# Upper norm at the front of a step, and the last block's dense part of MLP layer 1 computed in step 7, in a DLRM tower kernel

## The reference

```
x = layer_norm(dense @ Wd.T)                            # 128 per sample
y = layer_norm(einsum('bnd,ed->bne', e, Ws))            # 26 rows of 128
y = layer_norm(einsum('bne,pn->bep', y, Wsi))           # 32 per e
T = concat([x, y^T])                                    # 33 rows of 128
Z = T @ T^T ; Zflat = lower triangle of Z               # 528
z = layer_norm(Zflat @ Wl.T)[:, :384]                   # "upper" layer
h = relu(concat([z, dense]) @ W_top1 + b_top1)          # 384 + 256 -> 512
h = relu(h @ W_top2 + b_top2)                           # 512 -> 256
out = h @ W_top3                                        # 256 -> 1
```

## Time and profile before

| what | value |
|---|---|
| three executions | 182.54, 183.28, 187.37 us; median 183.28 |
| the profiled execution | 184.72 us; span from the first to the last instruction 182.9 us |
| mean granted TensorE clock in it | 0.944 |
| TensorE busy | 148.9 us (81% of the span), weight loads 105.9 |
| VectorE, ScalarE, GpSimd busy | 117.3, 85.9, 105.0 us |
| chain of work that ended last | GpSimd 36%, TensorE 34%, issue 14%, ScalarE 6%, DMA 5%, VectorE 3% |

### The profile page before, as it was taken

The page is one execution under the profiler, slowest core; times in us unless marked ns, Lnnn a source line. Parts: engine busy times, 40 slices in busy tenths (PEclk is TensorE's granted clock), DMA queues, the critical chain, the costliest instruction groups (busy, mean ns, idle before and its releaser), DMA issues.

```text
span 182.9 us, 4658 instructions
## 1 busy us (share of the span) xinstructions
PE 148.9 (81%) x1865; PEld 105.9 (58%) x1865; DVE 117.3 (64%) x279; ACT 85.9 (47%) x229; POOL 105.0 (57%) x108
## 2 busy tenths in 40 slices
PE   0474584658994979968896999999699999998995
PEld 0363262444452558635566977765398865596674
DVE  3799508794959999992969069968942898600000
ACT  3001324572634776752655256638604764522262
POOL 2778778787878787778777877788774000000000
PEclk9998869995899999999997899999969999999999
DMA  5714241325186633321255313212452102422000
GB/s 128 220 24 110 50 135 35 82 27 195 34 249 127 80 63 44 60 54 27 53 76 71 48 28 56 56 29 57 68 78 41 34 0 48 61 36 34 0 4 0
DMA packets 38520, 12.01 MB, mean 66 GB/s; under 512 B 34113, under 2 KB 35265, under 8 KB 38498
## 3 DMA queue, kind: packets, MB, share of 16 engines
q1 hardware_dynamic: 33586, 8.24, 20.2%
q0 software_dynamic: 3328, 3.41, 10.8%
q10 hardware_dynamic: 1584, 0.05, 0.5%
HBM read 9.46 MB, written 2.23 MB: 64 GB/s over the span
## 4 chain that ended last, share of the span: by engine, by line
POOL 36%; PE 34%; issue 14%; ACT 6%; DMA 5%; DVE 3%; SPq 1%; ACTq 0%
POOL rows L302 36%; PE pV L341 4%; PE pU L381 4%; PE pU L408 4%; PE pU L422 3%; PE pT L351 3%; PE pA L325 2%; PE pU L434 2%; PE pA L381 2%; PE pZ L364 2%; DMA zr<-zscr 1%; DMA rows<-in_tables,idx 1%; PE pA L318 1%; DMA idx_in<-in_index 1%; ACT ujunk L615 1%
## 5 line engine op out<-in xcount | busy, mean ns | idle before, releaser
L302 POOL DMA_INDIRECT rows<-in_tables,idx x104 | 104.7, 1007 | 34.3 <-issue 31.4
L756 DVE TENSOR_TENSOR prod<-pA,rows 128x384 f32<-128x384 f32 (+1 forms) x16 | 9.4, 591 | 28.8 <-PE pA L325 28.8
L780 DVE TENSOR_TENSOR t<-pT,bias 128x512 f32<-128x512 f32 x32 | 20.6, 684 | 4.3 <-PE pT L351 4.3
L584 ACT ACTIVATE t<-t 128x512 f32<-128x512 f32 x32 | 19.5, 629 | 7.4 <-DVE t L780 7.1
L795 DVE TENSOR_TENSOR T<-t,trs 128x512 f32<-128x512 f32 x32 | 22.2, 694 | 1.1
L318 PE MATMUL pA<-const,rows 128*128 128x128 f32 x52 | 9.0, 288 | 15.8 <-DMA rows<-in_tables,idx 15.8
L341 PE MATMUL pV<-wexp,srow 128*64 128x192 f32 (+4 forms) x256 | 21.4, 313 | 0.0
L786 DVE TENSOR_REDUCE tss<-t 128x16 f32<-128x512 f32 x32 | 20.4, 677 | 0.1
L325 PE MATMUL pA<-gbd,rowsT 128*128 128x128 f32 x104 | 17.5, 311 | 3.6 <-ACT rowsT L567 3.5
L364 PEld LDWEIGHTS pZ<-T 128*32 128x32 f32 x1024 | 12.2, 112 | 12.3 <-issue 9.8
L341 PEld LDWEIGHTS pV<-wexp,srow 128*64 128x64 f32 x256 | 16.4, 145 | 4.9 <-issue 2.7
(11 more groups left out here) (153 smaller groups left out, 214.0 us busy)
## 6 DMA issues: line engine op xcount, KB each, us to landing
zscr<-zs SPq DMA_DIRECT2D x16, 128.0 KB
rows<-in_tables,idx POOLq DMA_INDIRECT x104, 2.5
wl_sb<-in_wl SPq DMA_DIRECT2D x5, 256.0 KB, 2.9
w_sb<-in_w SPq DMA_DIRECT2D x5, 256.0 KB
dense_sb<-in_dense_t SPq DMA_DIRECT2D x1, 512.0 KB, 4.7
w_sb<-in_w SPq DMA_DIRECT2D x1, 512.0 KB, 4.5
zr<-zscr SPq DMA_DIRECT2D x3, 96.0 KB
const<-in_consts SPq DMA_DIRECT2D x1, 263.0 KB, 3.2
```

The source lines that it names most:

```text
L302: pool.indirect_dma_start(out=rows[:, j, h * D:(h + 1) * D], out_offset=None, in_=tables, in_offset=bass.IndirectOffsetOnAxis(ap=idx[:, 2 ...
L584: a.activation(t2[:, h], t1[:, n % 2, h], ACT.Square).then_inc(t_sq, 1)
L780: v.tensor_tensor(t1[:, n % 2, h], pT[h][:].rearrange("p (a b) -> p a b", b=PJ), bias[:].unsqueeze(1).to_broadcast([P, US, PJ]), ALU.add). ...
```

## The change

Eight edits, which compute the same result:
- In steps 9 and 13 VectorE's `upper_inverse` goes to the front of the step, ScalarE's `upper_scaled` ahead of `mixed`, TensorE's `turn` ahead of `interact`, and ScalarE's `upper_turned` ahead of `interactions`.
- In every step VectorE's `biased` is split: first half, `scaled_rows`, second half.
- In step 7 TensorE computes the dense part of layer 1 for block 3 into pU (`dense_ahead`), behind b1p; VectorE copies it to hd in SBUF; the first upper layer waits for the copy.
- `hidden1_dense(LAST)` goes; the last block's `hidden1` starts its sums itself.
- VectorE adds hd to these sums (`hidden_sum`, into hs), and the last relu1 reads hs in place of PSUM.
- In step 16 TensorE's part 1 of the upper layer of block 2 moves behind the embedding and the interactions of unit 14, with 2 and 3; parts 4 and 5 move behind the interactions of unit 15.
- ScalarE copies the interactions of unit 15 ahead of the norm and the scaling of block 2.

```
@@ PE @@
-                        pe.wait_ge(b1_ready, 1)
+                        pe.wait_ge(hd_sb, 1)
...
+            def dense_ahead():
+                pe.wait_ge(b1_ready, 1)
+                for m in range(H1 // P):
+                    for c in range(USED // P, NK):
+                        got = mm(pU[:, P * m:P * (m + 1)], w1_sb[:, c, P * m:P * (m + 1)],
+                                 dense_sb[:, c - USED // P, P * LAST:P * (LAST + 1)], start=c == USED // P, stop=c == NK - 1)
+                got.then_inc(hd_done, 1)
...
                 if k == LAST:
+                    pe.wait_ge(zs_sb, NU)
+                    pe.wait_ge(t1_sb, 2 * NU)
...
-                                     start=False, stop=c == USED // P - 1, skip_group_check=True)
+                                     start=c == 0, stop=c == USED // P - 1)
...
                 if n < NU:
                     gram(n)
+                if n == 7:
+                    dense_ahead()
...
-                if n == NU:
-                    upper(LAST - 1, [1])
                 if n:
                     embed(n - 1)
...
+                if (k := block_at(n, MLP)) is not None:
+                    turn(k)
...
                 if (k := block_at(n, MLP)) is not None:
-                    turn(k)
                     hidden1_dense(k)
...
                 if n == NU:
-                    upper(LAST - 1, [2, 3, 4, 5])
+                    upper(LAST - 1, [1, 2, 3])
             interact(NU - 1)
+            upper(LAST - 1, [4, 5])
             hidden1_dense(LAST - 1)
             turn(LAST - 1)
-            hidden1_dense(LAST)
             hidden1(LAST - 1)
@@ ACT @@
                 for m in range(H1 // P):
-                    if m == 0 or k == LAST:
-                        act.wait_ge(h1_done, H1 // P * k + (m + 1 if k == LAST else H1 // P))
-                    a.activation(h1[:, m, :], hidden_part(k, m), ACT.Relu, bias=b1p[:, m:m + 1]).then_inc(h1_sb, 1)
+                    got = hidden_part(k, m)
+                    if k == LAST:
+                        act.wait_ge(hs_sb, m + 1)
+                        got = hs[:, P * m:P * (m + 1)]
+                    elif m == 0:
+                        act.wait_ge(h1_done, H1 // P * (k + 1))
+                    a.activation(h1[:, m, :], got, ACT.Relu, bias=b1p[:, m:m + 1]).then_inc(h1_sb, 1)
...
+                if (k := block_at(n, MLP)) is not None:
+                    upper_scaled(k)
                 if n:
                     mixed(n - 1)
-                if (k := block_at(n, MLP)) is not None:
-                    upper_scaled(k)
...
+                if (k := block_at(n, MLP)) is not None:
+                    upper_turned(k)
                 if n >= 2:
                     interactions(n - 2)
-                if (k := block_at(n, MLP)) is not None:
-                    upper_turned(k)
...
+            interactions(NU - 1)
             upper_norm(LAST - 1)
             upper_scaled(LAST - 1)
-            interactions(NU - 1)
             x_row(LAST)
@@ DVE @@
+            def hidden_sum():
+                for m in range(H1 // P):
+                    dve.wait_ge(h1_done, H1 // P * LAST + m + 1)
+                    v.tensor_tensor(hs[:, P * m:P * (m + 1)], hidden_part(LAST, m), hd[:, P * m:P * (m + 1)],
+                                    ALU.add).then_inc(hs_sb, 1)
...
             for n in range(NU + 1):
+                if (k := block_at(n, MLP)) is not None:
+                    upper_inverse(k)
                 if n < NU:
                     row_variance(n)
-                if (k := block_at(n, MLP)) is not None:
-                    upper_inverse(k)
+                if n == 7:
+                    dve.wait_ge(hd_done, 1)
+                    v.tensor_copy(hd[:], pU[:]).then_inc(hd_sb, 1)
                 if n:
-                    biased(n - 1)
+                    biased(n - 1, 0)
                 if n < NU:
                     scaled_rows(n)
                 if n:
+                    biased(n - 1, 1)
                     variances(n - 1)
                     normalised(n - 1)
...
             upper_inverse(LAST)
+            hidden_sum()
```

More of the change, by code:

```diff
@@ L120, in build @@
         b1p = sb("b1p", [P, H1 // P])
+        hd = sb("hd", [P, H1])
+        hs = sb("hs", [P, H1])
         xstat = sb("xstat", [P, NBLK, 6])
@@ L196, in build @@
         w1_ready, b1_done, b1_ready = map(sem, ["w1_ready", "b1_done", "b1_ready"])
+        hd_done, hd_sb, hs_sb = map(sem, ["hd_done", "hd_sb", "hs_sb"])
         gathered = [sem(f"gathered{i}") for i in range(NU)]
@@ L400, in hidden1_dense @@
                     pe.wait_ge(t1_sb, 2 * NU)
-                if k == LAST:
-                    pe.wait_ge(zs_sb, NU)
-                    pe.wait_ge(u_sb, LAST)
                 if k == 0:
@@ L408, in hidden1_dense @@
                         mm(hidden_part(k, m), w1_sb[:, c, P * m:P * (m + 1)], dense_sb[:, c - USED // P, P * k:P * (k + 1)],
-                           start=c == USED // P and (m == 0 or k == LAST), stop=False, skip_group_check=True)
+                           start=c == USED // P and m == 0, stop=False, skip_group_check=True)
             def hidden1(k, part=range(USED // P)):
@@ L773, in scaled_rows, with biased @@
                                 ers[:, 0:2 * count].unsqueeze(2).to_broadcast([P, 2 * count, D]), ALU.mult).then_inc(s_sb, 1)
-            def biased(n):
-                if n >= 2:
+            def biased(n, h):
+                if n >= 2 and h == 0:
                     dve.wait_ge(t_sb, 2 * (n - 1))
-                for h in range(2):
-                    dve.wait_ge(y_done, 2 * n + h + 1)
-                    v.tensor_tensor(t1[:, n % 2, h], pT[h][:].rearrange("p (a b) -> p a b", b=PJ),
-                                    bias[:].unsqueeze(1).to_broadcast([P, US, PJ]), ALU.add).then_inc(t1_sb, 1)
+                dve.wait_ge(y_done, 2 * n + h + 1)
+                v.tensor_tensor(t1[:, n % 2, h], pT[h][:].rearrange("p (a b) -> p a b", b=PJ),
+                                bias[:].unsqueeze(1).to_broadcast([P, US, PJ]), ALU.add).then_inc(t1_sb, 1)
             def variances(n):
```

## The result

The changed kernel takes 189.9 us in the median of four runs (189.23 to 191.59); the kernel before, timed beside it, takes 183.62 us (182.54 to 187.37). The ratio is 1.0385 with a 95% interval of 1.0303 to 1.0468. The forecast was 185.2 us with a range up to 187.8.

The account below looks back on a forecast made before the run. Gathers set the earliest step starts; from about 100 us the chain is TensorE work, with a VectorE and ScalarE detour. Terms 0.75 + 0.4 - 0.1 + 0.6 + 0.3 = +1.95 us gave 185.2 us against 183.28, range 182.0 to 187.8.

Parts of the forecast that it names:

- Cost 0, hidden by that wait: Step 7: the 16 dense matmuls moved there cost nothing, hidden by step 8's wait for its rows.
- the cover: Before step 8: 2.68 us idle waiting for rows, called nearly used up; without it the step-7 work costs about 2.7 us.
- I leave the two clock falls as they are: Steps 9 and 13: the forecast keeps both falls of TensorE's clock; step 13's costs 1.6 us.
- Rival (b): Step 13: the stall closes, znT starts before 131.8, kernel faster at 181.1 us, half form 183.7; together 20%.
- the two terms: Steps 13 and 9: dense matmuls later by +0.75 us and +0.4 us.
- un displaces nothing: Step 9: ScalarE waited for the mixing matmuls before vsb, so only the split counts, +0.4 us.
- The second square in front of znT: Step 13, ScalarE: the second half's square delays znT from 131.81 to 132.55; TensorE idles some 2.2 us.
- Step 16, -0.1 us: Last embedding: srow of unit 15 comes 0.6 us earlier, mix gains 0.3, the embedding 0.1; bounds -0.3 to 0.
- The end, +0.6 us: After the last interactions: znT is later and ScalarE's reads wait for it, +0.6 us; bounds +0.2 (TensorE alone) and +1.0.
- The sum on VectorE, +0.3 us: Last stretch: the last 128x128 sum before relu, 0.27 us plus hand-over, lies in the path; bounds 0.2 and 0.7.
- Rival (c): Behind 150 us: TensorE's clock falls once or twice more, slower at 186.9 or 188.5 us; 13%.
- My list of new gaps: TensorE idle 1.3 us before the last embedding, 1.4 before the last interaction, 0.9 before the L422 matmuls.

Follow-up runs that it names:

- e8: The whole change, split kept, with znT copied between the two squares in steps 9 and 13: 185.46 us, ratio 1.0108.
- e12: The whole change, split kept, with step 7's dense_ahead directly ahead of upper(0) and the hd copy behind the scaled rows: 187.01 us, ratio 1.0264.
- e1: The kernel before with only the last block's dense part moved to step 7, with the copy to hd and sums on VectorE: 186.27 us, ratio 1.0194.
- e4: The changed kernel with both halves of the bias sum ahead of the scaled rows again: 184.18 us, ratio 1.0064.
- e10: The kernel before with only the new end: 183.82 us against 184.51, ratio 1.0119 (0.9983 to 1.0256).
- e9: The kernel before with only the new order of steps 9 and 13 and znT copied ahead of both squares, old end: 181.92 us, ratio 0.9936.
- e7: The change without split or step-7 work, with znT copied ahead of both squares in steps 9 and 13: 182.29 us, ratio 0.9941.
- e5: The change without split or step-7 work, only the new orders of steps 9 and 13 and the end: 183.27 us against 183.22, ratio 1.0022.
- e11: e9 with ScalarE's two copies of the last interaction ahead of the norm's scaling, TensorE's order old: 181.32 us, ratio 0.9934.
- e2: The kernel before with only the bias sum split around the scaled rows, in every step: 188.24 us, ratio 1.0246.
- e6: e4 with dense_ahead directly ahead of upper(0) in step 7 and the hd copy behind the scaled rows: 183.53 us, ratio 1.0006.
- e3: The changed kernel with the last block's dense part back at the end, no sum on VectorE: 186.47 us, ratio 1.001.

## Why the prediction was wrong

**Step 7, "Cost 0, hidden by that wait": wrong.** Its own steps show how. I took b1p from the earlier trace rows at 76.20, and nothing else moved. In the change b1p stands on VectorE behind w1g and the last T, and these behind the roots on ScalarE; it comes at 77.54. (How late it is varies: 5.1 us into the step in the change and 5.2 in e8, 4.0 in e12, all with the split; 4.5 in e1 and e4, without it. So the split is not its only cause.) The copy rowsT on ScalarE was late too, by 1.08 us on TensorE. And dense_ahead put a wait in front of 16 matmuls, so TensorE stood still with all that followed. Waits and work came to 1.08 + 1.67 + 3.62 = 6.4 us, where I had counted some 2 (76.35 to 78.2), and before, the step had 2.68 us to spare: 6.4 - 2.7 = 3.7 us too much, close to the 3.1 us found. I wrote that the cover was "nearly used up, without it ~2.7 us", so the price stood in the text, but nothing was set against the cover: neither the changes that the other edits make to this step, nor a fall of the clock. So the term had three sizes wrong: the arrival of b1p (5.1 us into the step, counted as 3.4), the new matmuls (3.62 us, counted as some 2) and the wait for rowsT (1.08 us, counted as nothing).

And the cover is no fixed number. Five of the kernels below are the kernel before up to step 9, and only its execution differs: their wait for rows ahead of step 8 is 1.77 us (e10), 1.50 (e9), 0.22 (e7) and none (e5, e11), and b1p comes 3.5 to 4.5 us into step 7, where the one trace that I had read has 2.68 and 3.4. Step 8 in e10 and e5:

```profile
82.33 0.63 PE L322 MATMUL pA<-const,rows 128*128 128x128 f32 x4 [1.77 <-DMA rows<-in_tables,idx]
84.56 0.60 PE L322 MATMUL pA<-const,rows 128*128 128x128 f32 x4
```

By these waits 2 us of new matmuls would be hidden in some executions and not in others, even where nothing else changes. e1's cost agrees with this, but no run isolates it.

**"I leave the two clock falls as they are": wrong as a baseline, and this hid the main cost of the split.** The dense matmuls of steps 9 and 13, counted by order over all traces of this case:

| order | idle ahead of them (us) | ran slow | step with full clock | step with a fall |
|---|---|---|---|---|
| as before (before, e1, e10) | 1.41 to 1.42 | 4 of 6 | 9.6 to 9.7 | 11.3 to 11.4 |
| as before, split (e2) | 2.45 | 2 of 2 | | 12.6 to 12.7 |
| new, not split (e4, e5, e6) | 1.30 to 1.44 | 0 of 6 | 9.2 to 9.8 | |
| new, split (the change, e3, e12) | 1.77 to 2.15 | 4 of 6 | 10.4 to 10.7 | 11.4 to 12.3 |
| znT ahead of a square (e7, e8, e9, e11) | at most 0.50 | 0 of 8 | 7.9 to 9.6 | |

The falls are no fixed part of the kernel before: with the same order they were missing in two of six places. And the new order without the split shortens a step only where it spares it a fall: with full clock on both sides it takes 9.2 to 9.8 us against 9.6 to 9.7. The timed runs of e5 show no gain, so what it wins on average is small, and that the order itself keeps the clock up (0 of 6) is suggested and not shown. What the split adds is clearer: at full clock about 0.9 us a step (e12 against e4 and e6), and 1.0 to 1.5 us more with a fall, which is what makes the change so much slower than e4 in these two steps. Rival (b) named the right lever, znT held by the second square, but it expected the change to pull it. Against the kernel before, whose trace had both falls, the two terms came to +0.8 in step 13 (forecast +0.75) and +1.0 in step 9 (forecast +0.4). That the first fits is partly luck, as both traces happen to have the fall. (A slip in the starting point: 136.78 - 133.6 is 3.2 us of lateness, and the idle time and the fall make 3.0 of it, not all of 3.1.) In step 9 "un displaces nothing" failed: un stands ahead of vsb there too, and rowsT is late as well (0.35 us of TensorE's time). The wait for vsb:

```profile
96.73 1.13 PE L355 MATMUL pT<-vsb,wscg 64*128 64x512 f32 x4 [0.39 <-ACT vsb L592]
```

**The second square in front of znT: right, and shown.** un, vsb, the second bias sum and znT came in the order and nearly with the distances given; TensorE idled for 1.79 us where I said 2.2. e2 adds the stall (2.45 us), e8 removes it (0.48 us) with everything else kept. Rival (b) asked for znT ahead of 131.8 and a closed stall; the change did not do this. The stall closes in e9 and shrinks to 0.48 us in e8.

**Step 16, -0.1 us: wrong sign.** The last embedding comes 8.7 us behind step 15's transposes, before 8.1. I counted srow of unit 15 as half a sum earlier. It was not earlier at all: it starts 5.2 us behind step 15's transposes before and after, since the last T of the unit before, and with it the row variance, moved back by as much as srow moved forward. The row before and the row after:

```profile
149.83 0.56 DVE L771 TENSOR_TENSOR srow<-rows,ers 128x384 f32<-128x384 f32 x1
153.57 0.56 DVE L788 TENSOR_TENSOR srow<-rows,ers 128x384 f32<-128x384 f32 x1
```

I also left out what stands in front of vsb on ScalarE. In step 16 that is both squares, the zs copies and the roots of unit 14, and the split makes them all late. The same event in e4 and in e8, which differ in the split here (ScalarE rows of the timeline; step 15's transposes at 144.07 and 144.05):

```profile
151.28 0.57 ACT L592 COPY vsb<-pV 128x512 f32<-128x512 f32 x1
```

```profile
152.10 0.57 ACT L592 COPY vsb<-pV 128x512 f32<-128x512 f32 x1
```

The split costs 0.8 us here. In every trace with the split the last embedding stands 8.66 to 8.67 us behind the transposes, in e4 7.83 us. So the split, whose purpose was an earlier srow, gained nothing in this stretch that could be set against its price.

**The end, +0.6 us: right in mechanism, too large.** The reads on ScalarE's queue left right behind the start of znT (167.97 and 167.91), as I read from the earlier trace rows; SyncE's reads of the same write had left at 166.85. But the path is TensorE's: the block-2 matmuls start 0.57 us behind znT, and the upper ones follow without a wait. From the last interaction this is +0.3 us, my lower bound of +0.2 and not the +0.6 of the reads. The new end as a whole costs about 0.4 us with the step-7 work in (e4: 38.7 us from step 15 to the end, before 38.3) and 0.8 without it (e5 and e10 39.1); these numbers are from traces, and the timed runs of e10 don't settle it.
Of the Trainium skill I had weighed "Advanced Engine Details and Errata", section "Sequencer Loop", by which further engine instructions can be read and queued while the sequencer handles one. Here the reads did not get past a copy that still waited; the row of after agrees with the earlier trace rows.

**The sum on VectorE, +0.3 us: right.** One sum takes 0.29 us (forecast 0.27), the path grew by 0.3.

**Rival (c), more clock falls behind 150 us, did not happen:** the slices of the page show 9 there. This is the line of the page after:

```profile
PEclk9997897999996999889998799999969999999999
```

An additional fall did happen, in step 7, where I had set no gap at all. My list of new gaps came from the end alone. Of these the ones ahead of the last embedding (1.40 us) and the last interaction (0.96 us) are there, and no fall followed.

**What stays open.** e8, with the stalls of steps 9 and 13 mended, is still 1.3 us above e4; 0.8 of it is step 16, the rest may be step 7, and no run separates it. What the step-7 work costs inside the split change is 3.4 us by e3's median and more by its ratio; its place alone (e12) makes up 2.9 us of the medians. Only one trace was taken of each kernel, so the steps of two kernels also differ by what differs from one execution to the next. Nor do the runs tell why the clock falls in one execution and not in another with the same stall (below).

## What to carry to other kernels

Before an operation is split or slid on an in-order engine, list every instruction that stands behind the second half on that engine and on the ones that read it, and look for the one that the bound engine waits for. Here a single copy (znT, 0.46 us) stood behind it, and taking it out from behind was worth 4.4 us. Then ask whether the first half comes earlier at all once the loop has settled: here srow did not.

Work moved into "spare" time needs three looks: whether its input is ready when the spare time begins, how much of the cover the other edits of the same change have already used, and whether the cover is there in more than one execution (here 2.68 us in the trace that was read, and 0 to 1.77 us in five others). And if the kernel before has stalls that cost more than their length, a forecast that holds them fixed misses both what an edit could win and what it throws away.

The parts worth having are the front order with znT ahead of both squares, and the old end or zs first: e9 181.92 and e11 181.32 us, against 184.51 us of the kernel before in that batch. The ratios, 0.9936 and 0.9934, make that a gain of about 1.2 us: clear of 1, but small.

## What the hardware showed that was not expected

The length of a stall does not tell whether TensorE's clock falls. The dense matmuls of steps 9 and 13 ran slow (3.5 to 3.6 us for 16) after 1.42 us of idle time in the kernel before, and at full clock after 1.41 and 1.42 us in step 9 of e1 and e10, which have the same order of work there, and after 1.44 us in e5. Within one execution, e10, step 9 and step 13 differ:

```profile
97.04 2.05 PE L421 MATMUL pU<-dense_sb,w_sb 128*128 128x128 f32 x16 [1.42 <-ACT znT L641]
129.93 3.06 PE L421 MATMUL pU<-dense_sb,w_sb 128*128 128x128 f32 x16 [1.42 <-ACT znT L641]
```

After 1.79 us they ran slow in the change (3.06 us in step 9, part of them at full clock, and 3.58 us in step 13), and at full clock (2.05 us) after 1.77 and 1.79 us in e12. After at most 0.50 us they never ran slow (e7, e8, e9, e11: eight times of eight). In step 7 the fall followed an idle time of 1.67 us in the change, whereas the 2.68 us of the earlier trace rows were followed by none. The Trainium skill, "Perfetto Trace Analysis", section "Matmul Optimizations", asks for matmuls back to back because the engine scales its power with its utilization. The traces agree in that direction, but a stall of a given length cost between 0 and 1.6 us more than itself, depending on the execution.

With the new end, the first read on ScalarE's DMA queue leaves within 0.07 us of the start of the copy in front of it (167.97 behind 167.91, and so in all eight other traces with this end), and not before: SyncE's reads of the same write left 0.8 to 1.3 us earlier in each of them.

For sums on VectorE, 128x128 from PSUM took 0.29 us where the line through 4 and 512 columns gave 0.27.
